# Filling the attention rooms of a two-layer kernel: through a DRAM scratch, or straight from SBUF

## What is computed

```python
Q, K, V = (proj(Wq), proj(Wk), proj(Wv))       # X @ W.T as (batch, 16 heads, n, 16)
Q1, Q2 = jnp.split(Q, 2, axis=-1)              # 8 features each
K1, K2 = jnp.split(K, 2, axis=-1)
A1 = jnp.where(causal, jnp.einsum('bhnd,bhmd->bhnm', Q1, K1) * scaling, -jnp.inf)
A2 = jnp.where(causal, jnp.einsum('bhnd,bhmd->bhnm', Q2, K2) * scaling, -jnp.inf)
attn = jax.nn.softmax(A1, axis=-1) - lam * jax.nn.softmax(A2, axis=-1)
O = jnp.einsum('bhnm,bhmd->bhnd', attn, V)
```

## Time and profile before

| | us |
|---|---|
| Median of 3 runs | 543.09 |
| Lowest and highest | 539.36, 544.16 |
| The profiled execution's own time | 540.0 |
| Span of the profile | 538.0 |
| PE busy | 483.7 (90%) |
| DVE, ACT, POOL busy | 392.4, 288.0, 267.0 |

### The profile page before, as it was taken

The page is one execution under the profiler, slowest core; times in us unless marked ns, Lnnn a source line. Parts: engine busy times, 40 slices in busy tenths (PEclk is TensorE's granted clock), DMA queues, the critical chain, the costliest instruction groups (busy, mean ns, idle before and its releaser), DMA issues.

```text
span 538.0 us, 8610 instructions
## 1 busy us (share of the span) xinstructions
PE 483.7 (90%) x3104; PEld 232.8 (43%) x3104; DVE 392.4 (73%) x796; ACT 288.0 (54%) x460; POOL 267.0 (50%) x223
## 2 busy tenths in 40 slices
PE   4892788888999999998997999999997998999995
PEld 4641443443445354453344545444343444443442
DVE  2414741969988988659887888469988977876584
ACT  1431444146686553656674654647773485548732
POOL 6031313124584914617653357626656467438963
PEclk9997789999999999999999999999999999999999
DMA  8700489803068480202486146111485166202111
GB/s 282 262 2 19 119 121 127 144 7 101 1 161 101 106 113 5 78 21 60 117 128 117 40 63 96 43 60 40 136 138 85 25 106 114 79 5 79 40 39 41
DMA packets 48474, 46.03 MB, mean 86 GB/s; under 512 B 5200, under 2 KB 38064, under 8 KB 47792
## 3 DMA queue, kind: packets, MB, share of 16 engines
q1 hardware_dynamic: 48432, 45.48, 41.0%
HBM read 37.47 MB, written 7.60 MB: 84 GB/s over the span
## 4 chain that ended last, share of the span: by engine, by line
PE 56%; DVE 15%; DMA 7%; SPq 7%; POOL 5%; ACT 4%; issue 4%; POOLq 1%; DVEq 0%; ACTq 0%
PE bank L737 7%; PE bank L728 6%; PE bank L749 6%; DMA ka<-parts_scratch 6%; PE scores L769 5%; SPq L514 5%; DVE nmax L1271 5%; PE scores L763 4%; PE bank L824 4%; PE scores L679 3%; PE scores L702 2%; PE scores L655 2%; PE scores L664 2%; PE scores L658 2%; PE bank L837 2%
## 5 line engine op out<-in xcount | busy, mean ns | idle before, releaser
L1070 POOL TENSOR_TENSOR gb<-gb,wb 128x512 f32<-128x512 f32 x64 | 84.7, 1324 | 114.8 <-ACT gb L978 104.2
L1271 DVE TENSOR_REDUCE nmax<-scores 128x4 f32<-128x1024 f32 (+1 forms) x96 | 113.7, 1216 | 32.2 <-PE scores L769 31.7
L1063 POOL TENSOR_SCALAR_AFFINE_SELECT pk<-pk 128x512 f32<-128x512 f32 (+1 forms) x96 | 82.9, 872 | 62.3 <-ACT pk L991 61.5
L991 ACT ACTIVATE pk<-scores 128x1024 f32<-128x1024 f32 x96 | 95.6, 1024 | 27.3 <-PE scores L769 27.1
L975 ACT ACTIVATE gt<-bank,bgh 128x512 f32<-128x512 f32 (+1 forms) x68 | 46.8, 688 | 62.6 <-PE bank L728 54.7
L737 PE MATMUL bank<-xnt,wu 128*128 128x512 f32 x128 | 69.2, 622 | 2.4 <-DVE h L1250 2.4
L728 PE MATMUL bank<-xnt,wg 128*128 128x512 f32 x128 | 68.7, 618 | 0.0
L749 PE MATMUL bank<-h,wd 128*128 128x512 f32 x128 | 66.8, 615 | 0.1
L1243 DVE SCALAR_TENSOR_TENSOR h<-gt,gb 128x512 f32<-128x512 f32 x64 | 49.6, 775 | 17.1 <-POOL gb L1070 12.6
L1250 DVE SCALAR_TENSOR_TENSOR h<-bank,bu,h 128x512 f32<-128x512 f32 x64 | 48.1, 751 | 17.3 <-PE bank L737 15.4
L763 PE MATMUL scores<-mask_h,ident_h 64*128 64x256 bf16 (+2 forms) x384 | 37.5, 273 | 12.3 <-DMA ka<-parts_scratch 8.2
(11 more groups left out here) (191 smaller groups left out, 732.3 us busy)
## 6 DMA issues: line engine op xcount, KB each, us to landing
wb<-wt_scratch SPq DMA_DIRECT2D x64, 256.0 KB, 4.1
parts_scratch<-parts SPq DMA_DIRECT2D x48, 128.0 KB, 2.4
qa<-parts_scratch SPq DMA_DIRECT2D x16, 192.0 KB
ka<-parts_scratch SPq DMA_DIRECT2D x16, 192.0 KB
qa<-parts_scratch SPq DMA_DIRECT2D x16, 128.0 KB
ka<-parts_scratch SPq DMA_DIRECT2D x16, 128.0 KB
x<-in_x SPq DMA_DIRECT2D x4, 256.0 KB, 2.7
ha<-in_wkq SPq DMA_DIRECT2D x1, 1024.0 KB, 5.2
```

The source lines that it names most:

```text
L991: A(dst.rearrange("p (h m) q -> p m h q", m=2), pairs[pair_of(step)][:, :, :].rearrange("p m (h q) -> p m h q", q=cols), ACT.Exp, scale=SC ...
L1063: pool.affine_select(out=dst, in_=dst, compare_op=ALU.is_ge, fill=0.0, base=0, pattern=[[0, heads], [1, P]], channel_multiplier=-1).then_i ...
L1070: pw(gb[:, c % 2, :], gb[:, c % 2, :], wb[:, k % 2, j % 2, :], ALU.mult).then_inc(s_ga_done, 1)
L1271: V.tensor_reduce(dst, src, AX, ALU.max, negate=True).then_inc(s_nmax_done, 1)
```

## The change

The scratch goes. `fetch` copies blocks of 8 rows straight from `parts` into the rooms: 24 DMAs of 64 KB per batch, part after part, each set waiting for its own part only. For this the columns of the query and key weights are put in another order on the host (`rooms`), so that in `parts` a half f is a softmax m and the partition is feature * 16 + head; 128 partitions of `parts` are then 8 rows of 16 heads. The step store does nothing any more. ACT's queries1 waits for both fetches of the chunk before in place of the stores.

```diff
-QK_IN = 16 * 2 * 6
+QK_IN = 16 * 4 * 6
+BLOCKS = (((0, 3, 5), (1, 4), (2,)), ((2, 4, 5), (1, 3), (0,)))
...
-                    elif kind == "store":
-
-                        for n in range(2):
-                            for a in range(3):
-                                done, name = ((s_part1, "part1"), (s_part2, "part2"), (s_part3, "part3"))[a]
-                                for f in range(2):
-                                    r = a if n == 0 else 2 - a
-                                    sp.wait_ge(done, at(c, name, 2 * n + f + 1))
-                                    dst = t["parts_dram"][c, n, f * 2 * GH:(f + 1) * 2 * GH, :, r * DH:(r + 1) * DH, :]
-                                    sp.dma_start(dst, parts[:, a, 2 * n + f, :]).then_inc(s_parts_stored, 16)
                     elif kind == "fetch":
                         b = rest[0]
-                        sp.wait_ge(s_parts_stored, at(c, "parts_stored", 16 * 12))
                         if c:
                             sp.wait_ge(s_sc_ps, unit(c - 1, b, GROUPS - 1, 2) + 1)
                         else:
                             sp.wait_ge(s_rooms, 3)
-                        for n, dst in enumerate((qa, ka)):
-                            for m in range(2):
-                                row = m * HALF
-                                for width in (3, 2, 1):
-                                    first = 0 if n == 0 else 3 - width
-                                    src = t["parts_dram"][c, n, :, m, first * DH:(first + width) * DH, b * SEQ:(b + 1) * SEQ]
-                                    sp.dma_start(dst[row:row + width * DH, b, :, :],
-                                                 src.rearrange("h r t -> r h t")).then_inc(s_qk_in[b], 16)
-                                    row += width * DH
+                        for a in range(3):
+                            done, name = ((s_part1, "part1"), (s_part2, "part2"), (s_part3, "part3"))[a]
+                            for n, dst in enumerate((qa, ka)):
+                                for m in range(2):
+                                    sp.wait_ge(done, at(c, name, 2 * n + m + 1))
+                                    for block in BLOCKS[n][a]:
+                                        row = m * HALF + block * DH
+                                        sp.dma_start(dst[row:row + DH, b, :, :],
+                                                     parts[:, a, 2 * n + m, b * SEQ:(b + 1) * SEQ]).then_inc(s_qk_in[b], 16)
...
                     if c and name == "queries1":
-                        act.wait_ge(s_parts_stored, at(c - 1, "parts_stored", 16 * 12))
+                        for b in range(CB):
+                            act.wait_ge(s_qk_in[b], c * QK_IN)
...
+    def rooms(w):
+
+        return w.reshape(P, HEADS, 2, DH).transpose(0, 2, 3, 1).reshape(P, -1)
...
-        "wq1": v["L1_attn_Wq"].T, "wk1": v["L1_attn_Wk"].T, "wv1": v["L1_attn_Wv"].T,
+        "wq1": rooms(v["L1_attn_Wq"].T), "wk1": rooms(v["L1_attn_Wk"].T), "wv1": v["L1_attn_Wv"].T,
```

More of the change, by code:

```diff
@@ L344, in build @@
         s_part3 = sem("part3")
-        s_parts_stored = sem("parts_stored")
         s_qk_in0 = sem("qk_in0")
@@ L391, in build @@
                    xnt1_sb=1, router_ps=1, rl_done=1, rexp_done=1, w_done=1, wt_ps=1, wt_sb=1, wt_stored=16,
-                   qk_ps=4, qk_rest=4, part1=4, part2=4, part3=4, parts_stored=16 * 12, v_ps=2, v_sb=2,
+                   qk_ps=4, qk_rest=4, part1=4, part2=4, part3=4, v_ps=2, v_sb=2,
                    max_ps=CB * UNITS, nmax_done=CB * UNITS, mp_done=CB, mrow_ps=CB, mrow_sb=CB, mrow_in=CB * MROWS_IN,
@@ L1330, in l0_and_l1_kernel @@
     t["out"] = out
-    t["parts_dram"] = nc.dram_tensor("parts_scratch", (CHUNKS, 2, HEADS, 2, 3 * DH, CHUNK), BF16, kind="Internal").ap()
     t["wt_dram"] = nc.dram_tensor("wt_scratch", (CHUNKS, E1, CHUNK), F32, kind="Internal").ap()
```

## The result

The changed kernel takes 581.5 us (median of 4 executions, 578.5 to 595.9) against 543.6 for the kernel before. The ratio is 1.069, with a 95% interval of 1.063 to 1.075. The profiled execution took 582.2 us, its span is 580.3. Some executions of any of these kernels are slowed as a whole, here that of 595.9 us; medians include them, ratios and their intervals do not.

What follows compares the result with a forecast made beforehand. PE, busy 90% of the span, was taken as the bound. Fetches of 24.4 us would delay its first uses by 20.6 us in total, other effects cancelling: 543 + 20 = 563 us for the median, range 542 to 600.

Steps and rivals of the forecast that it cites:

- What bounds the kernel, and where to look: PE, 90% busy, sets the end; only L763's waits for ka, 8.2 us, can change; stores, reordered weights, ACT's wait give 0.
- The pace of a fetch: Fetch into qa and ka: 0.94 us per transfer, SP pushed back, last landing after 2.8 us, 24.4 us in all.
- The sign that I named for the step to fall: On SP's queue: issues staying at 0.6 to 0.8 us, with the last transfer landing 3 us after its issue.
- the signs for the forecast: L763 waits at three or four places, 3 to 9 us each, over 25 total; issues near 0.9 us; under 80 GB/s.
- The cause behind the pace: Windows at 70 and 51 GB/s with DMA share 0.90 and 0.95 were read as transfers filling only 8 partitions.
- "Hidden" at chunk 1, batch 0: Fetch starts at 151.22, where the stores had been, and ends at 175.6, before PE's use at 178.97: no loss.
- "+0.1" at chunk 2, batch 1: Fetch ends at 340.05 against PE's first use at 339.90, a delay of 0.1 us.
- "I let these cancel.": PE's lower clock after longer stops, +0 to +5 us, set against shrinking waits for DVE, ACT and POOL, -2 to -5.
- the two-port pace: Rival: 51 GB/s throughout the fetch, 1.28 us per transfer, +79 us, 622 us; middle near 600, chance 0.22.
- The issue-bound cases: Rivals where SP's issuing sets the fetch: 0.81 us each, 551 us, chance 0.20; 0.64 us each, 537 us, chance 0.13.
- the "not slower" rival: Fetch runs at SP's issue price, 0.64 us per transfer; PE's waits fall 5.6 us, 537 us; chance 0.13.
- the rule of the sum: A fetch lasts 23 times the pace per transfer plus 2.8 us from issue to landing of the last.

Runs made afterwards that it cites:

- run 3: The kernel before, scratch and stores kept, each fetch of 24, 16 and 8 rows cut into transfers of 8 adjacent rows: 565.1 us, ratio 1.039.
- runs 1 and 2: The changed kernel with each transfer's 8 rows spread at a stride of 6 (539.1 us, ratio 0.992) or 2 (536.8 us, 538.3 repeated, ratio 0.989).

## Why the prediction was right, and where it was not

The forecast was 563 us in a range of 542 to 600, slower by over 1% with a chance of 0.77; 581.5 were measured, 18 us above the forecast and inside the range. By its steps:

*What bounds the kernel, and where to look.* Right. The change shows at the wait of L763 (L752 now) and nowhere else among PE's waits. The stores' removal gave nothing, the reordered weights nothing, and ACT's new wait does not appear.

*The pace of a fetch.* 24.4 us from first issue to first use were forecast. The seven places with a wait give 24.1, 25.0, 26.6, 20.1, 30.3, 26.0 and 26.8 us, 25.5 in the mean. The number was good, but its two parts were not, and that their errors cancelled was luck. I had SP pushed back to 0.94 us per issue and the last transfer landing after 2.8 us. SP was hardly pushed back (0.61 us, nearer to the store's price than to that of minus), and in the fetch shown above the last one landed after 9.95. That the queue takes more of the small transfers before it holds SP is not shown. In run 3, where SP issues a small one in 0.26 us at the least, it is held (a median of 0.66 into ka); so here its own slower issuing may be all that kept it from being held. The sign that I named for the step to fall, issues at 0.6 to 0.8 us with the last landing after 3, was met in its first half only. Of the signs for the forecast, under 80 GB/s and over 25 us of waits held; an issue median near 0.9 us, three or four places and at most 9 us each did not (0.61, seven, 1.65 to 10.75).

*The cause behind the pace* was argued in the prediction, from single microseconds at 51 and 70 GB/s; runs 1 and 2 show it. With size, count, source and price of issuing unchanged (a median of 0.612 to 0.613 us in all), the rows alone decide: 8 adjacent partitions are a narrow door, and 8 of 16 are a wide one. "SBUF — State Buffer", section "Door 1: The DMA port swizzle", of the Trainium skill gives each four neighbouring partitions one port; by this rule 8 adjacent rows reach two ports and 8 of 16 reach four. The runs agree with it in direction; what a port moves was not measured by itself, so that ports are the reason is not shown. By an estimate from that page's figure a transfer would have taken 1.20 us in steady flow; the trace gives 25.5 us per fetch, which less some 3 us of latency, over 24, are 0.94. The other rule cited, "DMA: Bandwidth & Descriptors", section "Why a DMA increments its semaphore by 16 and not by 1", would have 8 engines carry each of these transfers in runs 1 and 2 as well. No view shows the engines of a transfer. The transfers keep up with SP in runs 1 and 2, so the number of engines that carry them was not the limit.

*"Hidden" at chunk 1, batch 0.* I let its fetch begin at 151.22, where the stores had been. It began at 159.57: SP waits at that step for the last score matmul of the chunk before (L505 then, L494 now), 4.7 us by the view of SP's waits, whose release I had not looked up. Before, this wait was covered by the stores, which were issued until 158.9 and then waited for until 162.1. PE stood for 1.65 us there; with its start that much later, the fetch of the sum would have ended some 1 us after PE's use. This is the smallest miss, and the plainest: a step whose wait is removed has other waits, and the last of them sets the start.

*"+0.1" at chunk 2, batch 1.* It became 5.92 us. SP, not pushed back, issued two pairs of wb and the rows of minus from 347.14 on, while the fetch was still in the queue. Its transfers then shared the engines with them, where I had thought of SP as held until the fetch was nearly done. This fetch took 30.3 us, the longest of the seven; that the sharing made it so is argued and not tested.

*"I let these cancel."* This is the step that made most of the difference in size. The growth of the stops was forecast at 20.6 us and measured at 28.9, and to it came 13.6 us of PE at the lower clock, where I had 0 to 5, set against a gain of 2 to 5 by the others catching up. There was no gain: PE's other waits are what they were. What I had as a correction of zero was a third of the loss.

*The rivals.* The truth lies between the forecast and the two-port pace. The issue-bound cases would have come true with other rows: runs 1 and 2 give the time of the "not slower" rival, 537 to 539 us, with 0.61 us per issue. It had the waits fall by 5.6 us, though, and they fell by 1.4 to 1.8, to 6.4 to 6.8. That rival was rightly conditioned (from 0.70 us per transfer down), only that its condition was a matter of 8 row numbers. Two of the rivals' terms are off by a little: by the rule of the sum, 23 transfers and 2.8 us, a fetch at 1.28 us takes 32.2 us and not 32.4, and one at 0.64 takes 17.5 and not 17.1. Neither moves a rival's time by more than 2 us.

Where did the expected gain of the change go? With spread rows the two ways can be compared: 538.3 us direct, 532.5 through the scratch. The direct way saves the stores, which cost nothing on the path, and pays 24 issues of 0.61 us per batch (15.4 us) where the other pays 12 (8.8 us). So with spread rows in both kernels the edit as such costs about 6 us. This rests on two runs of four executions, made in different sets. The adjacent rows of small transfers cost the changed kernel another 43, and the adjacent rows of the old transfers cost the kernel before 11. What stays open: what filling the stops would give in the median, and why the rows matter, by ports or otherwise.

## What to carry to other kernels

Ask of each DMA that fills only a few partitions of SBUF whether they are neighbours, and try rows spread with a stride where the layout is free; here a stride of 2 turned a kernel slower by 7% into one faster by 1%, and made the kernel before faster by 2.3%. Count issues as well as bytes, since SP took 0.6 us for each transfer here, and don't give them to an engine that computes. And price a longer stop of PE with the lower clock behind it: here it was 13.6 us on top of 28.9 us of stops.

## What was unexpected of the hardware

- Into adjacent rows the low DMA pace comes with a high DMA share (0.58 at 67 GB/s); into rows 2 apart it was 0.30 at 82. Over the whole kernel the same 41904 packets took 35.1% and 25.9% of the engines' time. The share alone doesn't say that an engine moves anything.
- SP's issue of a transfer depends on its form. Where it is not held, it takes 0.26 to 0.4 us for DRAM into adjacent rows, 0.59 to 0.70 for DRAM into strided rows, 0.61 for SBUF into 8 rows whether adjacent or strided, 0.77 for the three rows of minus.
- Executions of the changed kernel, with its narrow fetch, scatter (570 to 596 us in eight); the four of the scratch kernel with spread rows lie within 0.4%, and its clock was 0.984 in all four.
- The ACT queue took 0.625 us per issue, and ACT's next activation came only after ten of them in a row (6.66 us idle).
